# Residual rows, ones, third norm, table order and last unit of an attention and mixture-of-experts kernel

## The reference

```python
x = x + layernorm(attn(layernorm(x)))
x = x + layernorm(moe(layernorm(x)))
# attn: two residual steps, both with softmax over squared distances
x = x + token_diffusion(ln1(x)) * gamma1      # 16 heads of 16, 512 tokens against 512
x = x + channel_diffusion(ln2(x)) * gamma2    # 8 heads of 32 channels against 32
# moe: 8 experts, the two largest of a softmax over logits weigh their outputs
out = sum_top2(weight * (gelu(x @ w1[e] + b1[e]) @ w2[e] + b2[e]))   # 256 -> 1024 -> 256
```

## Time and profile before

| | |
|---|---|
| time, median of 3 runs | 1094.52 us |
| lowest and highest | 1088.45 and 1095.66 us |
| profiled execution | 1096.26 us |
| its span in the trace | 1093.80 us |
| mean granted TensorE clock | 0.96 of full speed |
| busy: PE, weight loads, DVE, ACT, POOL | 980.5, 663.2, 696.7, 713.2, 430.4 us |
| moved by DMA | 171.10 MB, 156 GB/s over the span |

### The profile page before, as it was taken

One profiled execution on the slowest core, in us unless ns is written; L12 is line 12 of the kernel. 1 busy time (PEld: TensorE's weight loads), 2 busy tenths in 40 slices (PEclk: granted clock), 3 DMA queues, 4 the chain that ended last, 5 costly groups with the idle time before them and its releaser, 6 DMA issues.

```text
span 1093.8 us, 16766 instructions
## 1 busy us (share of the span) xinstructions
PE 980.5 (90%) x5468; PEld 663.2 (61%) x5468; DVE 696.7 (64%) x1883; ACT 713.2 (65%) x1090; POOL 430.4 (39%) x357
## 2 busy tenths in 40 slices
PE   5699999999999999969879997999999999989950
PEld 3223544545354454524578886888888888878850
DVE  5154376573946656364696689566766776768847
ACT  2587867766776776646746664577666777667835
POOL 5121030332314132223343446745555445445435
PEclk8799999999999999989989999999999999999985
DMA  7655625528073584842413442765665645567739
GB/s 269 140 156 151 237 55 169 177 71 275 16 241 89 161 293 152 275 158 73 169 37 109 118 121 59 232 188 146 151 160 132 168 129 122 124 177 214 205 45 291
DMA packets 57694, 171.10 MB, mean 156 GB/s; under 512 B 10384, under 2 KB 26896, under 8 KB 51728
## 3 DMA queue, kind: packets, MB, share of 16 engines
q1 hardware_dynamic: 38698, 137.99, 38.3%
q0 software_dynamic: 18768, 31.76, 15.0%
q10 hardware_dynamic: 150, 0.41, 0.2%
HBM read 98.55 MB, written 71.57 MB: 156 GB/s over the span
## 4 chain that ended last, share of the span: by engine, by line
PE 61%; DVE 20%; ACT 6%; issue 6%; POOL 4%; DMA 3%; DVEq 0%; ACTq 0%; POOLq 0%; SPq 0%
PE PH L1747 14%; PE PO L971 6%; PE PS L988 6%; PE PB L1051 6%; PE PY L1777 5%; PE PB L1777 4%; ACT E L595 3%; PE PA L1038 3%; PE PY L1782 3%; PE PY L1778 3%; DVE ST L200 2%; PE PB L1778 2%; DVE HP L1688 2%; DVE ON L742 2%; PE PB L1112 1%
## 5 line engine op out<-in xcount | busy, mean ns | idle before, releaser
L595 ACT ACTIVATE E<-PS,VV 128x1024 f32<-128x1024 f32 x256 | 270.6, 1118 | 73.1 <-PE PS L988 70.2
L1747 PE MATMUL PH<-XP,W1P 128*128 128x512 f32 (+1 forms) x1104 | 232.7, 369 | 15.1 <-DVE HP L1688 12.1
L1747 PEld LDWEIGHTS PH<-XP,W1P 128*128 128x128 f32 x1104 | 185.3, 192 | 55.7 <-DVE HP L1688 16.3
L1517 POOL DMA_INDIRECT choice_rows<-Y,DI x78 | 126.9, 1627 | 114.4 <-DVE Y L1648 83.7
L988 PE MATMUL PS<-OPB,OPA 102*128 102x512 bf16 x512 | 140.7, 390 | 14.5 <-DMA OPA<-norm_parts 7.9
L1688 DVE TENSOR_TENSOR HP<-PH,HP 128x512 fp32r<-128x512 f32 x156 | 106.7, 686 | 64.3 <-ACT HP L1597 63.7
L1592 ACT ACTIVATE PH<-PH,B 128x512 f32<-128x512 f32 (+1 forms) x184 | 107.5, 596 | 57.7 <-PE PH L1747 48.5
L971 PE MATMUL PO<-E,VA 128*32 128x512 f32 x1024 | 143.8, 611 | 0.0
L988 PEld LDWEIGHTS PS<-OPB,OPA 102*128 102x128 bf16 x512 | 37.4, 98 | 161.2 <-ACT E L595 75.9
L473 POOL DMA_INDIRECT expert_rows<-PAY,SLOT x64 | 62.7, 979 | 158.0 <-issue 81.4
L1583 ACT CAST W2P<-WG 128x512 fp32r<-128x512 f32 x92 | 56.8, 621 | 104.3 <-PE PB L1778 63.1
(11 more groups left out here) (245 smaller groups left out, 1554.5 us busy)
## 6 DMA issues: line engine op xcount, KB each, us to landing
expert_rows<-ZERO SPq DMA_DIRECT2D x8, 4160.0 KB, 13.0
WG<-experts SPq DMA_DIRECT2D x23, 1152.0 KB, 5.6
WG<-experts SPq DMA_DIRECT2D x23, 1028.0 KB, 5.6
OPB<-q_parts SPq DMA_DIRECT2D x192, 64.0 KB
q_parts<-QP SPq DMA_DIRECT2D x48, 128.0 KB
OPA<-q_parts SPq DMA_DIRECT2D x31, 192.0 KB
choice_rows<-ZERO SPq DMA_DIRECT2D x1, 5120.0 KB, 14.3
X<-x SPq DMA_DIRECT2D x8, 512.0 KB, 7.4
```

The lines of the kernel that those rows point to most:

```text
L595: a.activation(E[:, s % 2, h, :, :], PS[:, u % 2, :, :], ACT.Exp, scale=vec("tau_t")[:, 4 * (s // 2) + h:4 * (s // 2) + h + 1]).then_inc(e ...
L1517: g.indirect_dma_start(out=ys, out_offset=IND(ap=DI[:, t % 3, i:i + 1], axis=0), in_=Y[:, t % 2, i, :], in_offset=None, compute_op=ALU.add ...
L1747: last = m.matmul(PH[:, u % BANKS, at:at + w], W1P[:, a, k * HID + c * P:k * HID + c * P + P], XP[:, o, k, 0:w], start=(k == 0 and (a, o) ...
```

## The change

Seven edits:

1. `residual`: GpSimd keeps two small copies and one small product (128x4), the negated mean times the root. ScalarE makes X1 in four activations of 128x256 with that scale and bias. It waits for `x1_added` and for GpSimd's product. MU is stored negated; VectorE's `proj` waits for four counts per batch.
2. The third norm's `chan_norm` stands ahead of `proj` at position 5 in the bodies that have `LATE_AT` (2 to 6), by a new table `FIRST_AT`.
3. VA's ones are written by ScalarE in two halves, ahead of its first step, rather than by one memset on GpSimd.
4. `fill_tables`: operations on constants stand in a first section at slot 26, the row numbers RI come before DUMP and the rest and have a semaphore of their own, for which unit 5's gather waits. DUMP is one operation, last. The second group of weight loads takes its slot from a constant, 63.
5. The last unit's second layer does steps 0 to 3 for both blocks, then 4 to 7 block by block; VectorE's `result` and GpSimd's `send` follow per block.
6. `second`'s first step waits for as many blocks of the unit before as the unit itself has.
7. Stage 3: VectorE's adds of the chunks from the sixth on come behind all statistics.

```diff
-LATE_AT = {0: ['chan'], 1: ['chan_add'], 4: ['chan_stats'], 5: ['chan_norm'], 7: ['z3t0'], ...
+FIRST_AT = {5: ['chan_norm']}
+LATE_AT = {0: ['chan'], 1: ['chan_add'], 4: ['chan_stats'], 7: ['z3t0'], ...
-           **{k: ... for k, n in {52: 1, 53: 1, 54: 1, 55: 1, 57: 1, 58: 1, 59: 1, 60: 1, 62: 2, 63: 2}.items()}}
+           **{k: ... for k, n in {26: 1, 52: 1, 53: 1, 54: 1, 55: 1, 57: 1, 58: 1, 59: 1, 60: 1, 62: 1, 66: 1}.items()}}
...
-                g.memset(VA[:, :, :, :, :], 1.0).then_inc(setup_pool, 1)
...
             def residual(b, par):
-                at_least(pool, x1_added, b)
                 mus, rss = SM2[:, 4, :], SM2[:, 5, :]
                 pool.wait_ge(rs_ready, b + 1)
+                at_least(pool, x1_ready, 4 * b)
                 g.tensor_copy(mus, MU[:, ds(C * b, C)]).then_inc(x1_links, 1)
                 g.tensor_copy(rss, RS[:, ds(C * b, C)]).then_inc(x1_links, 1)
-                pool.wait_ge(x1_links, 2 * b + 2)
-                g.tensor_tensor(X1[:, :, :], X[:, ds(C * b, C), :], mus.unsqueeze(2).to_broadcast([P, C, D]), ALU.subtract
-                                ).then_inc(x1_ready, 1)
-                pool.wait_ge(x1_ready, 2 * b + 1)
-                g.tensor_tensor(X1[:, :, :], X1[:, :, :], rss.unsqueeze(2).to_broadcast([P, C, D]), ALU.mult
-                                ).then_inc(x1_ready, 1)
+                pool.wait_ge(x1_links, 3 * b + 2)
+                g.tensor_tensor(mus, mus, rss, ALU.mult).then_inc(x1_links, 1)
...
+            for half in range(2):
+                a.activation(VA[:, half, :, :, :].rearrange("p c h d -> p (c h d)"), HALF[:, 0, 0:1].to_broadcast([P, C * H * 32]),
+                             ACT.Copy, scale=-2.0).then_inc(ones_ready, 1)
...
+            def residual(b, par):
+                at_least(act, x1_added, b)
+                act.wait_ge(x1_links, 3 * b + 3)
+                for c in range(C):
+                    a.activation(X1[:, c, :], X[:, ds(C * b + c, 1), :].rearrange("p a e -> p (a e)"), ACT.Identity,
+                                 scale=SM2[:, 5, c:c + 1], bias=SM2[:, 4, c:c + 1]).then_inc(x1_ready, 1)
...
     link(v.tensor_copy(RI[:, :, :], row))
+    dve.sem_inc(rows_known, 1)
...
-                pool.wait_ge(tables_ready, 1)
+                pool.wait_ge(begun["rows_known"], 1)
...
-                pe.wait_ge(y_ready, first_block(t))
+                pe.wait_ge(y_ready, first_block(t - 1) + min(blocks_of(t - 1), blocks_of(t)))
...
+                if t == NUNITS - 1:
+                    for c in range(HC // 2):
+                        second(t, c)
+                    for i in range(blocks_of(t)):
+                        for c in range(HC // 2, HC):
+                            second(t, c, [i])
+                    break
...
-            if i - LAG >= BY_STORE:
-                add(i - LAG)
-        for i in range(len(CHUNKS) - LAG, len(CHUNKS)):
+        for i in range(BY_STORE, len(CHUNKS)):
             add(i)
```

More of the change, by code:

```diff
@@ L97, in body @@
                 do["att"](b, par, pos, first)
-            for flag, at, of, of_par in ((post, POST_AT, b - 1, 1 - par), (late, late, b - 2, par), (early, EARLY_AT, b + 2, par),
+            for flag, at, of, of_par in ((late is LATE_AT, FIRST_AT, b - 2, par), (post, POST_AT, b - 1, 1 - par), (late, late, b - 2, par), (early, EARLY_AT, b + 2, par),
                                          (pre, PRE_AT, b + 1, 1 - par)):
@@ L678, in norm1 @@
                 v.tensor_scalar(var[:, 1, :], MV[:, :, 1], 1.0 + EPS, EPS * EPS, ALU.mult, ALU.add).then_inc(var1_ready, 1)
-                early.did(v.tensor_copy(MU[:, ds(C * b, C)], MV[:, :, 0]))
+                early.did(v.tensor_scalar_mul(MU[:, ds(C * b, C)], MV[:, :, 0], -1.0))
                 early.wait()
@@ L919, in vector_program @@
             do["begin"] = begin
-            sections = fill_tables(nc, dve, table_links, tables_ready, COUNT, TAKEN, const,
+            sections = fill_tables(nc, dve, table_links, rows_known, tables_ready, COUNT, TAKEN, const,
                                    OT[:, :, :].rearrange("p g n -> p (g n)"), tables)
@@ L1276, in fill_begun, with fill_tables @@
     dve.sem_inc(begun_ready, 1)
-def fill_tables(nc, dve, table_links, tables_ready, COUNT, TAKEN, const, free, tables):
+def fill_tables(nc, dve, table_links, rows_known, tables_ready, COUNT, TAKEN, const, free, tables):
     v, ALU, AX = nc.vector, mybir.AluOpType, mybir.AxisListType
@@ L1300, in link @@
         dve.wait_ge(table_links, linked[0])
+    unit, offset, bounds, steps = take(S), take(S), take(2, VE + 1), take(3, VE)
+    link(v.tensor_copy(unit, const("unit")))
+    link(v.tensor_copy(offset, const("offset")))
+    link(v.memset(bounds, 0.0))
+    link(v.tensor_copy(steps[:, 2, :], const("expert_steps")))
+    yield
     rows_of, more, base = COUNT[:, 0, :], take(NE), take(VE)
@@ L1336, in fill_tables @@
     yield
-    bounds, steps = take(2, VE + 1), take(3, VE)
-    link(v.memset(bounds, 0.0))
     link(v.scalar_tensor_tensor(bounds[:, 0, 1:], start, -2.0 * SUB, base, ALU.mult, ALU.add))
@@ L1344, in fill_tables @@
     link(v.tensor_tensor(steps[:, 0:2, :], bounds[:, :, 1:], bounds[:, :, 0:VE], ALU.subtract))
-    link(v.tensor_copy(steps[:, 2, :], const("expert_steps")))
     yield
@@ L1363, in fill_tables @@
     link(v.tensor_tensor(OK[:, :, :], row, limit.unsqueeze(2).to_broadcast(wide), ALU.is_lt))
-    yield
-    link(v.tensor_tensor(DUMP[:, :, :], row, limit.unsqueeze(2).to_broadcast(wide), ALU.is_ge))
-    link(v.tensor_tensor(DUMP[:, :, :], DUMP[:, :, :], const("dump")[:, 2 * BEGUN * HALVES:].rearrange("p (s i) -> p s i", s=S), ALU.mult))
     link(v.tensor_scalar(limit, limit, -1.0, None, ALU.add))
@@ L1374, in fill_tables @@
     link(v.tensor_copy(WI[:, LEFT_PAIRS:], expert[:, 2 * LEFT_PAIRS:]))
+    link(v.scalar_tensor_tensor(DUMP[:, :, :], OK[:, :, :], 0.0, const("dump")[:, 2 * BEGUN * HALVES:].rearrange("p (s i) -> p s i", s=S),
+                                ALU.is_equal, ALU.mult))
     dve.sem_inc(tables_ready, 1)
@@ L1759, in turn, with second @@
             last.then_inc(xt_full, 1)
-        def second(t, c):
+        def second(t, c, blocks=None):
             n, w = chunks_per_group(t), width(t)
+            blocks = range(blocks_of(t)) if blocks is None else blocks
             j = c // n
             if c == 0 and t >= 1:
-                pe.wait_ge(y_ready, first_block(t))
+                pe.wait_ge(y_ready, first_block(t - 1) + min(blocks_of(t - 1), blocks_of(t)))
             if c == 0 and t == 0:
@@ L1773, in second @@
                 pe.wait_ge(begun["late_free"], LATE_USES * B)
-            for i in range(blocks_of(t)):
+            for i in blocks:
                 at = j * WIDE + c % n * w + i * P
@@ L1784, in second @@
                                     stop=(c == HC - 1 and (a, o) == terms[-1]), skip_group_check=True)
-            if c % n == n - 1:
+            if c % n == n - 1 if len(blocks) == blocks_of(t) else c == HC - 1:
                 last.then_inc(y_region, 1)
@@ L1818, in stage3 @@
     BY_STORE = KEPT
-    LAG = 2
     sb, pb, sem = made
```

36 lines of the change are left out of this document (20 added, 16 removed).

## The result

The changed kernel takes 1115.09 us as the median, against 1092.85 us for the kernel before (six runs each). The ratio is 1.0195, its 95% interval 1.017 to 1.0221: slower by 20 to 21 us. One of the six was disturbed (2392.96 us) and is left out of the ratio; the other five lie at 1112.26 to 1117.67 us, with 1112.79 in the middle. The profiled execution took 1112.30 us with a span of 1110.5, against 1096.26 and 1093.80: 16.7 us of span.

A forecast was written before the change was run, and what follows sets the result against it. TensorE, busy 61.62 of 64.00 us in the body, was taken as the bound. Terms, chiefly +13.0 (wait) and +9.0 (clock), summed to +16.7 on 1096.3: 1113.0, or 1111 us for the median; range 1094 to 1122.

The forecast's parts named there:

- The wait at `qk1`: Bodies 2 to 6: X1's activations delay `qk0`'s copies, so TensorE waits 3.3 us at `qk1`.
- Rival B: Bodies: VectorE's late steps run earlier, X1 is in time, the 1.30 us wait vanishes; 1079 us, chance 0.10.
- What a body gives back: Bodies 2 to 6: of the 3.3 us wait, 2.6 per body stays as NF moves too; +13.0 in all.
- Rival C: Bodies 2 to 6: nothing of the wait is swallowed, clock at its worst, 30.5 rather than 22.0; 1120 us, chance 0.15.
- The clock: Bodies 2 to 6: granted clock falls behind the new `qk1` wait, 1.8 us per body, +9.0 in all.
- Rival A: Bodies 2 to 6: the wait comes but the clock doesn't fall, the 9.0 goes; 1102 us, chance 0.22.
- Ones by ScalarE: Lead-in: SQ no longer starts behind GpSimd's memset of VA; -1.7 us (0 to -3.5).
- Third norm ahead: Bodies in the loop: PAY out of the way while GpSimd makes the root gives some 0.2 us back per body.
- Start of stage 2: Unit 0: ScalarE's wait for `x1_added` between two gelus, less 1.7 from GpSimd's passes gone; +1.9 us (0 to +3.3).
- Pairs to singles: Change from pairs to singles: the 3.28 us wait may start earlier, work behind on GpSimd unchanged; 0 (-3 to +1.7).
- Last unit: Last unit: block 0 leaves earlier, second scatter starts at about 1057.6 rather than 1059.87; -2.2 us (0 to -3).
- Tables: Before unit 5's gather: about ten small VectorE steps leave the stretch behind the 5.85 us wait; -2.5 us (-1 to -5.5).

The follow-up runs named there:

- e5: Changed kernel with three extra unread 128x512 matmuls on TensorE ahead of the wait at `qk1` in bodies 2 to 6; 1105.06 us, ratio 1.0106.
- e3: Changed kernel with the old residual, two passes of 128x1024 on GpSimd, all other edits kept; 1096.10 us, ratio 1.0006.
- e10: The kernel before, unchanged, run for a second profile; its one run took 1100.24 us.

## Why the prediction was right

**The wait at `qk1`.** Forecast 3.3 us from the add's end, 2.08 for the activations and 0.38 of slack. Measured 3.71, 3.31, 3.73, 3.31 and 2.98 in bodies 2 to 6, with 2.08 for the activations. Rival B, which needed X1 early, is excluded: the add ended 3.7 us behind the exponentials' start as before.

**What a body gives back.** Forecast 2.6 of the 3.3; e5 shows 2.9. NF did move with `proj`, though not by the same amount as the forecast held: the transposes' wait shrank from 1.30 to 0.61. Five times 2.9 is 14.5, forecast 13.0. Rival C, which needed more than 5 us per body, falls too: it is 4.5.

**The clock.** Forecast 1.8 per body, measured 68.44 - 66.81 = 1.6. The clock fell in all five bodies, in body 2 for twice as long (6.8 us, not 3.4); of the +24.0 some 9.5 are left for it beside the waits, forecast 9.0. Rival A falls for these waits of 2.98 to 3.73 us. The forecast took it as settled by the one wait of 2.10 that did lower the clock, and that was weaker than it looked: in e3 waits of 2.34, 2.37 and 2.33 us did not. The Trainium skill's rule ("TensorE: Matmul & The Clock Gate", section "HAM oscillation — how this bites in real kernels"), that a wait recurring in each pass is paid for in each pass, agrees with the five passes of this kernel at 2.98 to 3.73 us. It does not with e3, whose wait of about 2.35 us recurred and was paid for in the first pass alone. The figure of under 1% in the Trainium skill (same page, section "What's actually happening"), which the prediction held against this term, is said of the warm-up at a kernel's start. So it was no bound for falls that recur, and no run here tests it.

**Body 1 and body 7.** +1.7 and -2.5 forecast, +1.7 and -3.2 measured. In body 7 the wait of 9.78 is now two, of 6.59 together:

```profile
494.52 1.94 PE L996 MATMUL PS<-OPB,OPA 102*128 102x512 bf16 x4 [4.07 <-ACT E L603]
498.99 1.11 PE L1135 MATMUL PA<-KT,PAY 128*128 128x128 f32 x4 [2.52 <-DVE PAY L857]
```

ScalarE is late with X1 there too, and its exponentials with it.

**Where single steps failed.**

- *Ones by ScalarE, -1.7.* SQ did start at QF, but TensorE's chain behind gained only 0.3 to 1.0. And the trace of before had a slow lead-in, which I took for the kernel's own: slow by 5.9 us at a place where the change has no hand. At unit 0's rows it was quick by some 3 in the same sense. The two leave 2.9 us, in the direction in which the median's 20 to 21 us differ from 16.7.
- *Third norm ahead, worth 0.2.* It is worth nothing with X1 on ScalarE and costs 1.4 per body with X1 on GpSimd. I looked at what PAY did in the gap behind the statistics only as a delay, not as work that filled GpSimd's 1.1 us for the root.
- *Start of stage 2, +1.9.* ScalarE's wait cost 2.1, as forecast to 0.2. The rows' landing, 3.0 us more, was not in the forecast, and the unchanged kernel shows it too (e10).
- *Pairs to singles, 0.* I held that the gather and scatters behind would bring it all back. The wait went, 3.0 us, and the half clock behind it, 1.0. Of that 2.6 came back by the end of the singles, the most of it at a wait of 3.11 us (before 1.79) some 23 us on:

```profile
1009.70 7.43 PE L1761 MATMUL PH<-XP,W1P 128*128 128x256 f32 x48 [3.11 <-DVE XP L1685]
```

- *Last unit, -2.2.* The second scatter came 1.5 earlier against TensorE's end, and from its start to the end of the program it took 0.6 more (34.5 against 33.9). I missed that the first scatter waits for the landing of the unit before's:

```profile
1074.16 1.55 POOL L1528 DMA_INDIRECT choice_rows<-Y,DI  x1 [2.48 <-DMA choice_rows<-Y,DI]
1076.02 1.55 POOL L1528 DMA_INDIRECT choice_rows<-Y,DI  x1 [0.31 <-issue]
```

- *Tables, -2.5, measured -3.2.* The wait went from 5.85 to 3.99, while the wait ahead of it grew from 0.45 to 1.06. The clock behind was low for 3.4 us instead of 6.8, which gave the other 1.9 and was not in the forecast.

## What to carry to other kernels

Work moved to an engine with room costs nothing by its length and a lot by its place: look up which operation stands behind it in that engine's order and who waits for that, and put the moved work behind the last operation that the bound engine needs, as late as its own reader allows. A wait that the moved work brings along (here for an add on a third engine) holds everything queued behind it.

Before counting gains against a profile, look at whether its granted clock in that stretch is a property of the kernel or of the execution; a second profile of the same kernel tells it for the price of one run. The same goes for a wait on a load: 0.18 us in one profile of the kernel before and 3.44 in the other.

## What the runs showed of the hardware

The same program had its clock at 0.50 for V's matmuls in one execution and at 1.00 in another, where TensorE's waits ahead of them were 2.27 and 0.33 us, against 1.39 and 0.33 us. With it stage 1 started 5.9 us later.

Whether a wait lowers the clock was not settled by its length alone: a wait of 2.10 us ahead of L1094 did, and in e3 one of 2.38 did while 2.34, 2.37 and 2.33 did not. All of 2.98 to 3.73 us at `qk1` did, and the half clock behind each cost 1.6 us in bodies 3 to 6.

A pair of VectorE multiplications of 128x256 took 3.03 to 3.33 us beside GpSimd's passes over 128x1024 in bodies 2 to 7 of the kernel before, and 0.76 without them, in every body of the changed kernel.

ScalarE filled 128x2048 with a constant in 1.85 us (3.69 for two), less than the 2.1 that I had taken.
